# Last tail of a fused attention and FFN block: projection with centred, gamma-scaled weights and the residual summed on TensorE

## The chip, the cores and the metric

The kernel runs on one core of one Trainium2 chip. The metric is the device time of one execution in microseconds. Three runs of the kernel before gave 428.54, 428.6 and 428.6 us, median 428.6.

## The reference

The input x has 2048 rows of 128 numbers; there are 16 heads of 8 numbers each. What is computed:

```
xn  = layernorm(x)                              # no gamma, no beta
q, k, v = split(xn @ w_qkv)                     # per head
w   = relu(q k^T / sqrt(8));  w = w / (sum(w) + 1e-6)
o   = (w v) @ w_out + b_out
y   = xn + o
x1  = x + (y - mean(y)) * rsqrt(var(y) + 1e-5) * gamma + beta
z   = layernorm(x1)
out = x1 + sqrt((z @ cos(theta'))^2 + (z @ sin(phi'))^2)
```

All is fp32. theta' and phi' are the weights with their noise added.

## The kernel before

The 2048 rows are 16 tiles of 128, four tiles to a chunk (`TPC` = 4, `NC` = 4). The kernel makes four passes, one for the 512 queries of each chunk. A pass has 4 head groups of 4 heads, and a group has 16 steps, one for each tile of keys: `score_step` computes four score tiles (L961) into two of three PSUM pairs `sc0` to `sc2`, ScalarE and VectorE take their ReLU into `w_buf` (`relu_step`, L533, L536, L686, L690), and two steps later `value_step` multiplies them with the values and a column of ones into `pv0` or `pv1` (L996).

What follows the attention of a chunk (division by the sums, output projection, residual, post norm, FFN, norm of its output) is spread over the next pass as hooks: pairs `((group, step), function)` in the lists `after_pass`, on each engine its own. Every engine runs its instructions in the order in which they are written, and engines meet only at semaphores. So (2, 4) in VectorE's list of pass 1 means: behind the ReLUs of step 4 of group 2.

The last chunk has no next pass. Its end is written out as a tail in halves of two tiles each (`Part(NC - 1, 0)` and `Part(NC - 1, 1)`, 256 columns), and the engines take turns on it: ScalarE copies the sums of values to `pv_sb` (L613), TensorE transposes them (`transpose_pv`), VectorE divides (`normalise`, L699 to L701), TensorE transposes back (`transpose_o`), ScalarE copies into `oT` (L557), TensorE projects (`project_out`, L1022). From there `residual` adds `xn` (L748; `xn` holds the normalised x with b_out already added by GpSimd, L438), `post_stats` takes statistics (L756), `post_inverse` makes 1 / (var + eps) (L763 to L766), ScalarE the root (`post_root`, L562), `times_gamma` makes (y - mean) * gamma (L772), and `first_residual` x1 = that * rs + x_sb (L782; GpSimd has put x - mean + beta in `x_sb`). Then TensorE transposes x1 (L1003) and multiplies with the FFN weights (L1051), ScalarE squares (L571), VectorE adds (L836), ScalarE takes roots (L581), VectorE adds x2 (L844), and SyncE's queue stores. Meanwhile GpSimd adds the mean back (`mean_again`, L457). Between the projections and the transposes of x1 TensorE runs 20 matmuls that nobody reads (`warm_up`, L922).

An object `Own` is an engine's wait on its own last write, by a semaphore, before it reads it.

Of the kernel before, what the change touches and what calls it, by code (L numbers as in the profile page):

```python
# [44 lines left out]
STEPS = G * NT  # L45
W_STEPS = 4
WARM_UP = 12
TAIL_WARM_UP = 20
PSUM_PAIRS = 3
LAG = 2  # L50
FIRST_BOTH_LATE = ((1, 11, 13, 15), (3, 8, 10, 12, 14), (0, 3, 8, 12), (3, 8, 11, 13))
# [29 lines left out]
def block_kernel(nc, x, w_qkv, w_out, b_out, gamma, beta, theta, phi, theta_noise, phi_noise, out):  # L81
# [3 lines left out]
    with ctx:  # L85
        def sb(name, shape, dt=F32):
            return ctx.enter_context(nc.sbuf_tensor(name, shape, dt))

        def sem(name):
            return ctx.enter_context(nc.semaphore(name))  # L90
# [40 lines left out]
        angles = sb("angles", [P, 4, D])  # L131
        turns = sb("turns", [P, 2, D])
        ffn_w = sb("ffn_w", [P, 2, D])
        averager = sb("averager", [P, P])
        stats = sb("stats", [P, NT, 6])
        mv = sb("mv", [P, NT, 2])
# [93 lines left out]
        mag_ready = sem("mag_ready")  # L230
        x2_ready = sem("x2_ready")
        stored = sem("stored")

        def k_turn(c):

# [2 lines left out]
        def chunk(c):  # L238
            return bass.ds(c * TPC, TPC)
# [47 lines left out]
        def row(v, d):  # L287

            return v[:, :].unsqueeze(1).to_broadcast([P, d, D])

        with nc.Block() as block:
# [97 lines left out]
            def _(pool):  # L389
# [45 lines left out]
                pool.wait_ge(consts_loaded, 64)  # L435
                pool.wait_ge(xT_done, NC + 1)
                for c in range(NC):
                    nc.gpsimd.tensor_tensor(xn[:, chunk(c), :], xn[:, chunk(c), :], row(bout_b, TPC),  # L438
                                            ALU.add).then_inc(xb_ready, 1)
# [21 lines left out]
                def finish(part):  # L461

                    mean_again(part)
                    for n, tiles, _ in part.pieces():
                        sl = slice(tiles.start, tiles.stop)
                        pool.wait_ge(sq_ready, n + 1)
                        nc.gpsimd.tensor_tensor(mag[:, sl, :], sq[:, sl, 0, :], sq[:, sl, 1, :],  # L467
                                                ALU.add).then_inc(sum_ready, 1)
                    pool.wait_ge(mag_ready, 2 * part.n + 2)
                    pool.wait_ge(mean_back, part.n + 1)  # L470
                    nc.gpsimd.tensor_tensor(x2[:, :, :], x2[:, :, :], mag[:, :, :], ALU.add).then_inc(x2_ready, 1)  # L471


                scale_o(0, G)
                finish(Part(0))
                for c in range(1, NC - 1):
# [12 lines left out]
            def _(act):  # L489
# [134 lines left out]
            def _(dve):  # L624
# [129 lines left out]
                def post_stats(part, src):  # L754
                    for t in part.all():
                        last = nc.vector.bn_stats(stats_p[:, t, :], src[:, t, :])  # L756
                    part.chain(last)

                def post_inverse(part, norm):

                    nc.vector.memset(spare[:, :], 0.0)
                    for t in part.all():
                        last = nc.vector.bn_aggr(mv_p[:, t, :], stats_p[:, t, :])  # L763
                    part.chain(last)
                    part.chain(nc.vector.tensor_scalar_add(iv_p[:, norm, part.sl()], mv_p[:, part.sl(), 1], LN_EPS))
                    nc.vector.reciprocal(iv_p[:, norm, part.sl()],  # L766
                                         iv_p[:, norm, part.sl()]).then_inc(iv_ready[norm], 1)
# [57 lines left out]
                dve.wait_ge(xb_ready, 2 * NC)  # L825
                dve.wait_ge(consts_loaded, 64)
                for c in range(1, NC):
                    run_pass(c, after_pass(c - 1)
                             + ([((3, 7), lambda: invert_sums(NC - 1, G - 1))] if c == NC - 1 else []))

                halves = [start_chain(Part(NC - 1, 0)), start_chain(Part(NC - 1, 1))]

                def tail_sum(part, i):
                    n, (t,), _ = part.pieces()[i]
# [25 lines left out]
            def _(pe):  # L860
# [58 lines left out]
                def warm_up(n):  # L919

                    for _ in range(n):
                        nc.tensor.matmul(pv[0][:, 0:P], ident[:, :], ident[:, :], start=True, stop=True)  # L922

                pe.wait_ge(ident_ready, 1)
                warm_up(WARM_UP)
# [129 lines left out]
                def after_pass(j):  # L1055
                    part = Part(j)
                    return [((0, 12), lambda: project_out(part)),
                            ((1, 11), lambda: transpose_x1(part)), ((2, 4), lambda: ffn(part, 0)),
                            ((2, 8), lambda: ffn(part, 1))]

                def run_pass(c, hooks):

                    for s in range(STEPS):
                        score_step(c, s)
                        if s < LAG and c > 0:
                            value_step(c - 1, STEPS - LAG + s)
# [22 lines left out]
                    value_step(NC - 1, s)  # L1089

                halves = [Part(NC - 1, 0), Part(NC - 1, 1)]
                for part in halves:
                    transpose_pv(part.half, part.pv_bank, part.all())
                for stage in (transpose_o, project_out):
                    for part in halves:
                        stage(part)
                warm_up(TAIL_WARM_UP)
# [27 lines left out]
```

## Time and profile before

| | us |
|---|---|
| median of 3 runs | 428.6 |
| the profiled execution | 428.66 |
| its span (first to last instruction) | 426.8 |
| busy TensorE in a stretch of 95 us, about a pass | 95.00 |
| last matmul of the attention to the end of the span | 16.0 |
| projection of the first half ready to x1 of the second half | 5.9 |

In the rows below, times are microseconds from the span's start, and a name such as L1022 is a line of the listing. PE is TensorE, PEld its weight loads, DVE VectorE, ACT ScalarE, POOL GpSimd. A busy time that stands before x4 is that of four instructions that overlap in part, so four durations sum to more than it.

### The profile page before, as it was taken

The numbers are of one execution on the slowest core, as the hardware profiler recorded it, in microseconds if no ns is written. First come the engines' busy times: TensorE is split into PE (matmuls) and PEld (weight loads), VectorE is DVE, ScalarE is ACT, GpSimd is POOL, SyncE is SP. The second block draws the span as 40 slices with busy tenths as digits, with TensorE's granted clock in tenths as the row PEclk, the third lists the DMA queues.
The fourth block names the chain that finished last, engine by engine and source line by source line (L and its number), as shares of the span: only waits on it lengthen the run. The fifth ranks groups of instructions, "written<-read, shape, count | busy, mean of one in ns | idle before, by whom it ended". The sixth has DMA issues, their size and how long they took to land.

```text
span 426.8 us, 9025 instructions
## 1 busy us (share of the span) xinstructions
PE 415.0 (97%) x3294; PEld 122.9 (29%) x3294; DVE 332.9 (78%) x659; ACT 339.1 (79%) x595; POOL 45.9 (11%) x57
## 2 busy tenths in 40 slices
PE   7899999999999999999999999999999999999985
PEld 6333222222222322222222322222222322222244
DVE  6775778777688898777778898777778898777857
ACT  2767878788788888888888888888888888888843
POOL 4794000000000000000101000000100000000201
PEclk9999999999999999999999999999999999999999
DMA  5117841001012100101011100101012000000200
GB/s 166 25 51 148 162 111 51 2 8 43 2 51 56 26 26 13 39 2 51 26 53 54 26 27 16 35 2 51 26 51 55 2 27 2 25 2 29 66 0 26
DMA packets 11134, 17.42 MB, mean 41 GB/s; under 512 B 3092, under 2 KB 4756, under 8 KB 10708
## 3 DMA queue, kind: packets, MB, share of 16 engines
q1 hardware_dynamic: 10948, 16.70, 14.6%
q8 instruction: 29, 0.48, 0.5%
q10 hardware_dynamic: 144, 0.13, 0.2%
q14 instruction: 13, 0.11, 0.1%
HBM read 3.86 MB, written 5.10 MB: 21 GB/s over the span
## 4 chain that ended last, share of the span: by engine, by line
PE 93%; DVE 3%; ACT 2%; DMA 1%; POOL 0%; issue 0%; DVEq 0%
PE pv L996 59%; PE sc L961 27%; PE pv L1051 1%; PE pv L893 1%; PE pv L902 1%; PE pv L914 1%; DMA x_sb<-x_dram 1%; PE pv L1022 1%; ACT w_buf L536 0%; PE pv L1003 0%; DVE stats L640 0%; ACT w_buf L533 0%; DVE x L782 0%; PE sc L1051 0%; PE sc L1003 0%
## 5 line engine op out<-in xcount | busy, mean ns | idle before, releaser
L996 PE MATMUL pv<-w_buf,v_sb 128*32 128x512 f32 x2048 | 272.4, 604 | 0.0
L686 DVE TENSOR_SCALAR w_buf<-sc 128x512 f32<-128x512 f32 x256 | 176.9, 691 | 73.8 <-PE sc L961 64.9
L533 ACT ACTIVATE w_buf<-sc 128x512 f32<-128x512 f32 x256 | 153.1, 598 | 67.0 <-PE sc L961 66.5
L536 ACT ACTIVATE w_buf<-sc 128x512 f32<-128x512 f32 (+1 forms) x256 | 183.7, 718 | 0.0
L961 PE MATMUL sc<-q_rep,k_rep 32*128 32x512 f32 x1024 | 134.0, 494 | 2.3 <-ACT w_buf L533 0.9
L690 DVE TENSOR_SCALAR w_buf<-sc 128x512 f32<-128x512 f32 x182 | 123.8, 680 | 1.3 <-PE sc L961 1.3
L961 PEld LDWEIGHTS sc<-q_rep,k_rep 32*128 32x128 f32 x1024 | 52.4, 181 | 216.6 <-ACT w_buf L533 175.9
L996 PEld LDWEIGHTS pv<-w_buf,v_sb 128*32 128x32 f32 x2048 | 40.4, 108 | 66.5 <-ACT w_buf L536 34.1
L451 POOL TENSOR_TENSOR oT<-o_raw,o_scale 128x512 f32<-128x512 f32 (+1 forms) x4 | 5.1, 1282 | 164.6 <-DMA o_scale<-inverse_dram 100.7
L467 POOL TENSOR_TENSOR mag<-sq 128x256 f32<-128x256 f32 x6 | 4.4, 730 | 77.5 <-ACT sq L571 77.5
L457 POOL TENSOR_TENSOR x<-x,mv 128x512 f32<-128x512 f32 (+1 forms) x5 | 4.4, 885 | 71.2 <-DVE x L782 71.2
L922 PE MATMUL pv<-ident 128*128 128x128 f32 x64 | 9.4, 316 | 1.5 <-POOL ident L392 1.5
L922 PEld LDWEIGHTS pv<-ident 128*128 128x128 f32 x64 | 9.1, 230 | 1.5 <-POOL ident L392 1.5
L471 POOL TENSOR_TENSOR x<-x,mag 128x512 f32<-128x512 f32 x3 | 3.8, 1283 | 52.7 <-ACT mag L581 52.7
L544 ACT COPY pv_sb<-pv 128x512 f32<-128x512 f32 x15 | 8.8, 585 | 0.2
L1051 PE MATMUL pv<-ffn_w,x1T 128*128 128x256 f32 x24 | 6.8, 405 | 0.0
L659 DVE TENSOR_TENSOR q_lo<-pv,q_hi 128x512 fp32r<-128x512 f32 x4 | 2.8, 692 | 4.3 <-ACT q_hi L505 4.3
L581 ACT ACTIVATE mag<-mag,iv_p 128x128 f32<-128x128 f32 x16 | 5.4, 398 | 0.0
L397 POOL MEMSET v_sb<- 128x1472 f32 x4 | 5.3, 1334 | 0.0
L438 POOL TENSOR_TENSOR xn<-xn,bout_b 128x512 f32<-128x512 f32 x4 | 5.1, 1284 | 0.0
L441 POOL TENSOR_TENSOR x_sb<-x_sb,beta_b 128x512 f32<-128x512 f32 x4 | 5.1, 1279 | 0.0
L782 DVE SCALAR_TENSOR_TENSOR x<-y,rs_p,x_sb 128x128 f32<-128x128 f32 x16 | 5.0, 367 | 0.0
(104 smaller groups left out, 136.1 us busy)
## 6 DMA issues: line engine op xcount, KB each, us to landing
pv_dram<-pv_sb SPq DMA_DIRECT2D x15, 256.0 KB, 2.0
q_rep<-q_hi SPq DMA_DIRECT2D x30, 64.0 KB, 2.1
q_rep<-q_lo SPq DMA_DIRECT2D x30, 64.0 KB, 2.1
k_rep<-k_hi SPq DMA_DIRECT2D x6, 256.0 KB, 4.1
k_rep<-k_lo SPq DMA_DIRECT2D x6, 256.0 KB, 5.3
x_sb<-x_dram SPq DMA_DIRECT2D x3, 256.0 KB, 3.9
o_raw<-pv_dram SPq DMA_DIRECT2D x3, 256.0 KB
o_scale<-inverse_dram SPq DMA_DIRECT2D x3, 256.0 KB
```

What stands on the lines that cost most here:

```text
L397: nc.gpsimd.memset(v_sb[:, :, heads, HD + 1:VW], 0.0).then_inc(v_pad, 1)
L438: nc.gpsimd.tensor_tensor(xn[:, chunk(c), :], xn[:, chunk(c), :], row(bout_b, TPC), ALU.add).then_inc(xb_ready, 1)
L533: nc.scalar.activation(w_buf[:, s % W_STEPS, 0, :], early[:, 0, :], ACT.Relu).then_inc(relu[0], 1)
L536: nc.scalar.activation(w_buf[:, s % W_STEPS, 2:2 + n, :], late[:, 0:n, :], ACT.Relu).then_inc(relu[0], 1)
L544: nc.scalar.copy(pv_sb[:, :], bank[:, :]).then_inc(pv_out, 1)
L581: last = nc.scalar.activation(mag[:, t, :], mag[:, t, :], ACT.Sqrt, scale=iv_p[:, 1, t:t + 1])
L686: nc.vector.tensor_scalar(w_buf[:, s % W_STEPS, 1, :], early[:, 1, :], 0.0, None, ALU.max).then_inc(relu[1], 2 if both else 1)
L690: nc.vector.tensor_scalar(w_buf[:, s % W_STEPS, 3, :], late[:, 1, :], 0.0, None, ALU.max).then_inc(relu[1], 1)
L922: nc.tensor.matmul(pv[0][:, 0:P], ident[:, :], ident[:, :], start=True, stop=True)
L961: last = nc.tensor.matmul(sc[buf][:, i % 2, :], k_rep[rows, g, k * P:(k + 1) * P], q_rep[rows, g, :], start=True, stop=True)
L996: last = nc.tensor.matmul(bank[32 * i:32 * i + 32, :], v_sb[:, k, HPG * g + i, :], w_buf[:, s % W_STEPS, i, :], start=(k == 0), stop=(k == ...
L1051: last = nc.tensor.matmul(bank[:, m * 2 * D:(m + 1) * 2 * D], x1T[:, t * P:(t + 1) * P], ffn_w[:, :, :].rearrange("p c d -> p (c d)"), sta ...
```

## The change

The tail of the last chunk is computed in another way. The mean over a row of the projection is linear in its input. So TensorE gets two other right sides: `wout_tail[0]`, w_out with each row's mean taken away, and `wout_tail[1]`, the same times gamma. `x_tail[0]` and `x_tail[1]` are the last chunk's xn plus centred bias, without and with gamma. A matmul of the identity with `x_tail` opens an accumulation (`tail_x`), and the projection adds to it. One sum (in `sc2`) gives the variance, and its statistics are taken by VectorE straight from PSUM; the other (in `pv0` and `pv1`) is the centred and scaled y, from which `tail_x1` makes x1 in one instruction for each tile. ScalarE takes the root of var + eps with eps as bias, and VectorE the reciprocal. The 20 matmuls of `warm_up` in the tail are gone. The small right sides are made ahead: the means of the rows by VectorE in pass 1 (`tail_means`, a hook at (2, 4)), the rest by GpSimd behind its work on chunk 0 (`centred_tail`), and GpSimd's add of b_out to chunk 3 is left out.

```diff
+                def centred_tail():
+                    last = chunk(NC - 1)
+                    pool.wait_ge(means_ready, 1)
+                    nc.gpsimd.tensor_tensor(wout_tail[:, 0, :], wout_sb[:, :], row_means[:, 0:1].to_broadcast([P, D]),
+                                            ALU.subtract).then_inc(wout_centred, 1)
...
+                    nc.gpsimd.tensor_tensor(x_tail[:, 0, :, :], xn[:, last, :], row(bias_tail, TPC),
+                                            ALU.add).then_inc(x_tail_centred, 1)
...
-                for stage in (take_oT, post_root, take_x1T):
+                def tail_root(part):
+                    act.wait_ge(tail_var, part.half + 1)
+                    nc.scalar.activation(std_p[:, part.sl()], mv_p[:, part.sl(), 1], ACT.Sqrt,
+                                         bias=eps_col[:, :]).then_inc(tail_std, 1)
...
+                def tail_means():
+                    own = Own(dve, means_own)
+                    nc.vector.tensor_reduce(row_means[:, 0:1], wout_sb[:, :], mybir.AxisListType.X, ALU.add)
+                    own(nc.vector.tensor_reduce(row_means[:, 1:2], bout_b[:, :], mybir.AxisListType.X, ALU.add))
+                    nc.vector.tensor_scalar_mul(row_means[:, :], row_means[:, :], 1 / D).then_inc(means_ready, 1)
...
+                def tail_stats(part):
+                    dve.wait_ge(proj_done, part.n + 1)
+                    for n, t in enumerate(part.all()):
+                        last = nc.vector.bn_stats(stats_p[:, t, :], part.y_bank[:, n * P:(n + 1) * P])
+                    own[part.half](last)
...
+                def tail_x1(part):
+                    dve.wait_ge(scaled_done, part.half + 1)
+                    own[part.half].wait()
+                    for n, t in enumerate(part.all()):
+                        last = nc.vector.scalar_tensor_tensor(
+                            out=x1[:, t, :], in0=pv[part.half][:, n * P:(n + 1) * P], scalar=rs_p[:, t:t + 1],
+                            in1=x_sb[:, bass.ds(part.j * TPC + t, 1), :].rearrange("p o d -> p (o d)"),
+                            op0=ALU.mult, op1=ALU.add)
+                    last.then_inc(x1_ready, 1)
+                    dve.wait_ge(x1_ready, part.n + 1)
...
-                for stage in (residual, lambda p: post_stats(p, y), lambda p: post_inverse(p, 0), times_gamma,
-                              first_residual, lambda p: post_stats(p, x1), lambda p: post_inverse(p, 1)):
+                first, second = halves
+                tail_stats(first)
+                tail_variance(first)
+                tail_stats(second)
+                tail_inverse(first)
+                tail_variance(second)
+                tail_x1(first)
+                tail_inverse(second)
+                tail_x1(second)
+                for stage in (lambda p: post_stats(p, x1), lambda p: post_inverse(p, 1)):
...
+                def tail_x(part, which, bank):
+                    nc.tensor.matmul(bank[:, 0:part.tiles * P], ident[:, :],
+                                     x_tail[:, which, part.sl(), :].rearrange("p t d -> p (t d)"),
+                                     start=True, stop=False)
...
```

On TensorE, from the transposes of the sums of values on, the order was this (`sc` and `pv` with their buffer's number):

```order
L1003 MATMUL sc0<-ident,pv_sb 128x128 x2
L1003 MATMUL sc1<-ident,pv_sb 128x128 x2
L1003 MATMUL sc0<-ident,o_sb 128x128 x2
L1003 MATMUL sc1<-ident,o_sb 128x128 x2
L1022 MATMUL sc2<-wout_sb,oT 128x128 x4
L922 MATMUL pv0<-ident 128x128 x20
L1003 MATMUL sc0<-ident,x1 128x128 x2
```

And the same place of the changed kernel, which has one row more ahead of the transposes:

```order
L1186 MATMUL pv0<-x_tail,ident 128x256
L1093 MATMUL sc0<-ident,pv_sb 128x128 x2
L1093 MATMUL sc1<-ident,pv_sb 128x128 x2
L1186 MATMUL sc2<-x_tail,ident 128x256
L1093 MATMUL sc0<-ident,o_sb 128x128 x2
L1093 MATMUL sc1<-ident,o_sb 128x128 x2
L1196 MATMUL sc2<-wout_tail,oT 128x128 x2
L1186 MATMUL sc2<-x_tail,ident 128x256
L1196 MATMUL sc2<-wout_tail,oT 128x128 x2
L1196 MATMUL pv0<-wout_tail,oT 128x128 x2
L1186 MATMUL pv1<-x_tail,ident 128x256
L1196 MATMUL pv1<-wout_tail,oT 128x128 x2
```

The second half's projection for the statistics now stands behind a matmul of 256 columns, and four projections and one more such matmul stand where the 20 unread ones were.

On VectorE, between the division (`o_sb`) and the statistics of x1, the order was this:

```order
L748 TENSOR_TENSOR y<-sc2,xn 128x256 x2
L756 BN_STATS stats_p<-y 128x6 x4
L761 MEMSET spare 128x1
L763 BN_AGGR mv_p<-stats_p 128x2 x2
L765 TENSOR_SCALAR iv_p<-mv_p 128x2
L766 RECIPROCAL iv_p<-iv_p 128x2
...
L772 SCALAR_TENSOR_TENSOR y<-y,mv_p,gamma_b 128x128 x4
L782 SCALAR_TENSOR_TENSOR x1<-y,rs_p,x_sb 128x128 x4
```

In the changed kernel the same place holds these:

```order
L889 BN_STATS stats_p<-sc2 128x6 x2
L895 BN_AGGR mv_p<-stats_p 128x2 x2
L889 BN_STATS stats_p<-sc2 128x6 x2
L901 RECIPROCAL rs_p<-std_p 128x2
L895 BN_AGGR mv_p<-stats_p 128x2 x2
L908 SCALAR_TENSOR_TENSOR x1<-pv0,rs_p,x_sb 128x128 x2
L901 RECIPROCAL rs_p<-std_p 128x2
L908 SCALAR_TENSOR_TENSOR x1<-pv1,rs_p,x_sb 128x128 x2
```

The adds of `xn` and the multiplications by gamma are gone, and the halves are interleaved in another way.

## Rows read from the trace of the kernel before

**Rows 1.** Page, part 1: busy time and share of the span
```profile
PE 415.0 (97%) x3294; PEld 122.9 (29%) x3294; DVE 332.9 (78%) x659; ACT 339.1 (79%) x595; POOL 45.9 (11%) x57
```

**Rows 2.** Stretches: busy us of each engine, then granted clock, DMA share, GB/s
```profile
310.00:405.00 95.00, 95.00 (x784) 25.52 (x780) 76.93 (x143) 79.88 (x139) 6.34 (x6) 1.00 0.10 29
411.00:413.60 2.60, 1.51 (x9) 0.90 (x9) 1.09 (x6) 0.87 (x3) 0.00 (x0) 1.00 0.00 0
413.60:419.20 5.60, 5.60 (x49) 5.42 (x48) 4.46 (x22) 0.77 (x3) 0.00 (x0) 1.00 0.02 3
```

**Rows 3.** Timeline of the tail, TensorE and ScalarE: start, us, engine, instructions
```profile
408.01 2.78 PE L996 MATMUL pv<-w_buf,v_sb 128*32 128x512 f32 x24
411.29 0.71 PE L1003 MATMUL sc<-ident,pv_sb 128*128 128x128 f32 x4 [0.49 <-ACT pv_sb L613]
413.21 0.41 PE L1003 MATMUL sc<-ident,o_sb 128*128 128x128 f32 x2 [0.16 <-DVE o_sb L701]
413.51 1.28 PE L1022 MATMUL sc<-wout_sb,oT 128*128 128x128 f32 x8
413.66 0.36 ACT L557 COPY oT<-sc 32x256 f32<-32x256 f32 x1 [0.20 <-PE sc L1003]
414.62 4.63 PE L922 MATMUL pv<-ident 128*128 128x128 f32 x40
420.51 1.89 PE L1051 MATMUL sc<-ffn_w,x1T 128*128 128x256 f32 x8
```

**Rows 4.** Timeline of VectorE in the tail
```profile
414.26 0.42 DVE L748 TENSOR_TENSOR y<-sc,xn 128x256 f32<-128x256 f32 x1 [1.19 <-PE sc L1022]
414.89 0.42 DVE L748 TENSOR_TENSOR y<-sc,xn 128x256 f32<-128x256 f32 x1 [0.21 <-PE sc L1022]
415.35 1.01 DVE L756 BATCH_NORM_STATS2 stats_p<-y 128x6 f32<-128x128 f32 x4
416.40 0.18 DVE L763 BATCH_NORM_AGGREGATE mv_p<-stats_p 128x2 f32<-128x6 f32 x1
416.50 0.15 DVE L763 BATCH_NORM_AGGREGATE mv_p<-stats_p 128x2 f32<-128x6 f32 x1
417.45 0.17 DVE L766 RECIPROCAL iv_p<-iv_p 128x2 f32<-128x2 f32 x1
417.54 1.12 DVE L772 SCALAR_TENSOR_TENSOR y<-y,mv_p,gamma_b 128x128 f32<-128x128 f32 x4
418.58 1.61 DVE L782 SCALAR_TENSOR_TENSOR x<-y,rs_p,x_sb 128x128 f32<-128x128 f32 x4
```

**Rows 5.** Chain of waits from x1 on: start, us, what
```profile
420.24 0.44 PE sc L1003 x2
420.68 1.31 PE sc L1051 x6
```

**Rows 6.** Line L782 in the tail: shortest, median and longest in ns
```profile
L782 DVE SCALAR_TENSOR_TENSOR x<-y,rs_p,x_sb x4: 343/348/700, 418.6 to 419.5; 128x128 f32<-128x128 f32 x4
```

**Rows 7.** Timeline of GpSimd, and of VectorE beside it
```profile
419.35 0.69 POOL L457 TENSOR_TENSOR x<-x,mv 128x256 f32<-128x256 f32 x1 [15.22 <-DVE x L782]
10.39 1.04 POOL L418 TENSOR_TENSOR xn<-xn,rstd 128x512 f32<-128x512 f32 x1
10.47 0.72 DVE L671 SCALAR_TENSOR_TENSOR k_rep<-k_head,low_rows,sc 128x512 fp32r<-128x512 f32 x1
23.21 4.04 POOL L433 TENSOR_TENSOR x_sb<-x_sb,mv 128x512 f32<-128x512 f32 x4
25.43 0.69 DVE L659 TENSOR_TENSOR k_lo<-pv,k_hi 128x512 fp32r<-128x512 f32 x1 [0.39 <-ACT k_hi L501]
```

**Rows 8.** Groups of the tail: busy us, mean ns, idle before
```profile
L562 ACT ACTIVATE rs_p<-iv_p 128x2 f32<-128x2 f32 x2 | 0.4, 204 | 3.4 <-DVE iv_p L766 3.4
L581 ACT ACTIVATE mag<-mag,iv_p 128x128 f32<-128x128 f32 x4 | 1.3, 391 | 0.0
L756 DVE BATCH_NORM_STATS2 stats_p<-y 128x6 f32<-128x128 f32 x4 | 1.0, 285 | 0.1
L1022 PE MATMUL sc<-wout_sb,oT 128*128 128x128 f32 x8 | 1.3, 300 | 0.0
L1051 PE MATMUL sc<-ffn_w,x1T 128*128 128x256 f32 x8 | 1.9, 380 | 0.0
```

**Rows 9.** Timeline around step (2, 4) of pass 1, and a VectorE reduction near the start
```profile
1.50 0.22 DVE L629 TENSOR_REDUCE low_rows<-ident 128x1 f32<-128x64 f32 x1 [1.50 <-POOL ident L392]
176.61 0.69 DVE L686 TENSOR_SCALAR w_buf<-sc 128x512 f32<-128x512 f32 x1 [0.15 <-PE sc L961]
178.57 0.51 PE L961 MATMUL sc<-q_rep,k_rep 32*128 32x512 f32 x4
179.11 0.69 DVE L686 TENSOR_SCALAR w_buf<-sc 128x512 f32<-128x512 f32 x1 [1.21 <-PE sc L961]
```

**Rows 10.** Timeline of GpSimd around its new work
```profile
203.43 1.28 POOL L471 TENSOR_TENSOR x<-x,mag 128x512 f32<-128x512 f32 x1 [17.55 <-ACT mag L581]
233.59 1.28 POOL L451 TENSOR_TENSOR oT<-o_raw,o_scale 128x512 f32<-128x512 f32 x1 [28.87 <-issue]
```

More of the change, by code:

```diff
@@ L47 @@
 WARM_UP = 12
-TAIL_WARM_UP = 20
 PSUM_PAIRS = 3
@@ L133, in block_kernel @@
         ffn_w = sb("ffn_w", [P, 2, D])
+        row_means = sb("row_means", [P, 2])
+        wout_tail = sb("wout_tail", [P, 2, D])
+        bias_tail = sb("bias_tail", [P, D])
+        x_tail = sb("x_tail", [P, 2, TPC, D])
+        eps_col = sb("eps_col", [P, 1])
+        std_p = sb("std_p", [P, TPC])
         averager = sb("averager", [P, P])
@@ L232, in block_kernel @@
         stored = sem("stored")
+        means_own = sem("means_own")
+        means_ready = sem("means_ready")
+        wout_centred = sem("wout_centred")
+        bias_centred = sem("bias_centred")
+        x_tail_centred = sem("x_tail_centred")
+        tail_ready = sem("tail_ready")
+        scaled_done = sem("scaled_done")
+        eps_ready = sem("eps_ready")
+        tail_var = sem("tail_var")
+        tail_std = sem("tail_std")
+        tail_own = [sem("tail_own0"), sem("tail_own1")]
         def k_turn(c):
@@ L437, in _ @@
                 for c in range(NC):
-                    nc.gpsimd.tensor_tensor(xn[:, chunk(c), :], xn[:, chunk(c), :], row(bout_b, TPC),
-                                            ALU.add).then_inc(xb_ready, 1)
+                    if c < NC - 1:
+                        nc.gpsimd.tensor_tensor(xn[:, chunk(c), :], xn[:, chunk(c), :], row(bout_b, TPC),
+                                                ALU.add).then_inc(xb_ready, 1)
                     pool.wait_ge(x_centred, c + 1)
@@ L471, in finish @@
                     nc.gpsimd.tensor_tensor(x2[:, :, :], x2[:, :, :], mag[:, :, :], ALU.add).then_inc(x2_ready, 1)
+                def centred_tail():
[3 more added lines that the diff above has]
+                                            ALU.subtract).then_inc(wout_centred, 1)
+                    nc.gpsimd.tensor_tensor(bias_tail[:, :], bout_b[:, :], row_means[:, 1:2].to_broadcast([P, D]),
+                                            ALU.subtract).then_inc(bias_centred, 1)
+                    pool.wait_ge(wout_centred, 1)
+                    nc.gpsimd.tensor_tensor(wout_tail[:, 1, :], wout_tail[:, 0, :], gamma_b[:, :],
+                                            ALU.mult).then_inc(tail_ready, 1)
+                    pool.wait_ge(bias_centred, 1)
+                    nc.gpsimd.tensor_tensor(x_tail[:, 0, :, :], xn[:, last, :], row(bias_tail, TPC),
+                                            ALU.add).then_inc(x_tail_centred, 1)
+                    pool.wait_ge(x_tail_centred, 1)
+                    nc.gpsimd.tensor_tensor(x_tail[:, 1, :, :], x_tail[:, 0, :, :], row(gamma_b, TPC),
+                                            ALU.mult).then_inc(tail_ready, 1)
+                nc.gpsimd.memset(eps_col[:, :], LN_EPS).then_inc(eps_ready, 1)
                 scale_o(0, G)
                 finish(Part(0))
+                centred_tail()
                 for c in range(1, NC - 1):
@@ L613, in _ @@
                     nc.scalar.copy(pv_sb[:, part.cols()], pv[1][:, part.cols()]).then_inc(pv_out, 1)
-                for stage in (take_oT, post_root, take_x1T):
+                def tail_root(part):
+                    act.wait_ge(tail_var, part.half + 1)
+                    nc.scalar.activation(std_p[:, part.sl()], mv_p[:, part.sl(), 1], ACT.Sqrt,
+                                         bias=eps_col[:, :]).then_inc(tail_std, 1)
+                act.wait_ge(eps_ready, 1)
+                for stage in (take_oT, tail_root, take_x1T):
                     for part in halves:
@@ L827, in _ @@
                 for c in range(1, NC):
-                    run_pass(c, after_pass(c - 1)
+                    run_pass(c, after_pass(c - 1) + ([((2, 4), tail_means)] if c == 1 else [])
                              + ([((3, 7), lambda: invert_sums(NC - 1, G - 1))] if c == NC - 1 else []))
                 halves = [start_chain(Part(NC - 1, 0)), start_chain(Part(NC - 1, 1))]
+                own = [Own(dve, tail_own[0]), Own(dve, tail_own[1])]
+                def tail_stats(part):
[3 more added lines that the diff above has]
+                    own[part.half](last)
@@ new lines, in tail_variance, with tail_inverse @@
+                def tail_variance(part):
+                    for t in part.all():
+                        last = nc.vector.bn_aggr(mv_p[:, t, :], stats_p[:, t, :])
+                    last.then_inc(tail_var, 1)
+                def tail_inverse(part):
+                    dve.wait_ge(tail_std, part.half + 1)
+                    own[part.half].later(nc.vector.reciprocal(rs_p[:, part.sl()], std_p[:, part.sl()]))
+                def tail_x1(part):
[8 more added lines that the diff above has]
+                    dve.wait_ge(x1_ready, part.n + 1)
@@ L917, in project_v, with warm_up @@
                     last.then_inc(v_done, 1)
-                def warm_up(n):
+                def warm_up(n, bank):
                     for _ in range(n):
-                        nc.tensor.matmul(pv[0][:, 0:P], ident[:, :], ident[:, :], start=True, stop=True)
+                        nc.tensor.matmul(bank[:, 0:P], ident[:, :], ident[:, :], start=True, stop=True)
                 pe.wait_ge(ident_ready, 1)
-                warm_up(WARM_UP)
+                warm_up(WARM_UP, pv[0])
                 transpose_first()
@@ L1091, in _, with project_tail @@
                 halves = [Part(NC - 1, 0), Part(NC - 1, 1)]
+                first, second = halves
+                def tail_x(part, which, bank):
+                    nc.tensor.matmul(bank[:, 0:part.tiles * P], ident[:, :],
+                                     x_tail[:, which, part.sl(), :].rearrange("p t d -> p (t d)"),
+                                     start=True, stop=False)
+                def project_tail(part, which, bank, done):
+                    if which == 0:
+                        pe.wait_ge(oT_ready, part.n + 1)
+                        pe.wait_ge(oT_three, 1)
+                    for n, t in enumerate(part.all()):
+                        last = nc.tensor.matmul(bank[:, n * P:(n + 1) * P], oT[:, t * P:(t + 1) * P],
+                                                wout_tail[:, which, :], start=False, stop=n == part.tiles - 1)
+                    last.then_inc(done, 1)
+                pe.wait_ge(tail_ready, 2)
+                tail_x(first, 1, pv[0])
                 for part in halves:
                     transpose_pv(part.half, part.pv_bank, part.all())
[L1094 to L1097, printed above, removed]
+                tail_x(first, 0, first.y_bank)
+                transpose_o(first)
+                transpose_o(second)
+                project_tail(first, 0, first.y_bank, proj_done)
+                tail_x(second, 0, second.y_bank)
+                project_tail(second, 0, second.y_bank, proj_done)
+                project_tail(first, 1, pv[0], scaled_done)
+                tail_x(second, 1, pv[1])
+                project_tail(second, 1, pv[1], scaled_done)
                 for part in halves:
```

2 lines of the change are left out of this document (1 added, 1 removed).

## The prediction

> **What bounds the kernel now.** I read the page's busy times first. TensorE is busy for 97% of the span, VectorE for 78%, GpSimd for 11% [rows 1]. Then the stretches: a whole pass shows 95.00 us of busy TensorE in 95 us at a granted clock of 1.00, so the passes are bound by TensorE, and work on other engines is free there as long as TensorE doesn't wait for it. The stretch 411.0 to 413.6 shows 1.51 us of 2.6 [rows 2]: from the last attention matmul on (408.01 + 2.78 = 410.79) the engines take turns. Third, the timeline of that tail. The projection of the first half is ready when VectorE's first add starts, at 414.26; VectorE then works, but for a wait of 0.21, to the end of L782 at 418.58 + 1.61 = 420.19 [rows 4]. TensorE shows as busy in that time, but 414.62 to 419.25 is the unread warm-up [rows 3]. So there VectorE alone sets the end. Behind it stands the chain of x1: transposes at 420.24, FFN matmuls at 420.68 [rows 5], the rest to the span's end at 426.8. That chain starts at the second half of x1, and the change doesn't touch it. What the change is worth is how much sooner than 420.19 that x1 is there.
>
> **The part that is replaced.** Before: 420.19 - 414.26 = 5.93 us. It holds two adds (414.26 to 415.31, with a wait for the second half's projection), four statistics (415.35 to 416.36), two variances with reciprocals (to 417.62), four multiplications by gamma and four L782 [rows 4].
>
> After, on VectorE, by the same rows. The start stays 414.26: the first projection needs the same `oT`, and what stands new ahead of it on TensorE is covered (below).
> - First statistics: four took 1.01 [rows 4] at 285 ns each [rows 8], a distance of (1.01 - 0.285) / 3 = 0.24, so 0.53 for two: to 414.79. Own wait 0.04 (416.36 to 416.40). Two aggregations 0.25 (416.40 to 416.65): 414.83 to 415.08.
> - Second statistics: they need the second projection. TensorE: L1022's last instruction of the first half starts about 413.90, for it lasts 275 ns and the add started at 414.26 some 0.09 behind its end. Instructions follow each other at 0.11 us for 128 columns (4.63 us less one duration, over 39) and at 0.216 for 256 columns (1.89 - 0.38 = 1.51 over 7) [rows 3, 8]; a matmul in fp32 is two instructions. So the identity matmul starts at 414.01, and the four instructions of the second projection at 414.44 to 414.76, ending at 415.04, seen by VectorE at 415.13. Before it was 414.89; now it is 0.24 later, yet VectorE is free only at 415.10. Statistics 415.13 to 415.66.
> - Reciprocal of the first half: 0.04 + 0.17, to 415.87. ScalarE's root has had since 415.08; it is not late.
> - Aggregation of the second half 415.80 to 416.05, laid over the reciprocal as L763 is laid over L766.
> - x1 of the first half: two instructions at a distance of 0.28 with 0.35 for the last (1.12 for four L772; 343 ns for L782 alone [rows 4, 6]), 0.63: 416.07 to 416.70.
> - Reciprocal of the second half 416.74 to 416.91, own wait, x1 of the second half 416.94 to 417.57.
>
> After: 417.57 - 414.26 = 3.31. The gain is 5.93 - 3.31 = 2.62 us.
>
> **Does TensorE keep up?** Behind the second projection come two scaled projections (4 instructions each) with an identity matmul between: first scaled one 414.87 to 415.47, needed at 416.07; the second starts at 415.73 and ends at 416.33, needed at 416.94. It has 0.5 us of room. The 20 warm-up matmuls are no loss of work, and the transposes of x1 no longer queue behind them. The identity matmul ahead of `transpose_pv` falls into the idle 0.49 us before 411.29 [rows 3], of which it needs 0.43; the one ahead of `transpose_o` into the time in which VectorE divides.
>
> **The price of what no row shows.** Statistics with a PSUM source: the nearest rows are adds and multiply-adds with one PSUM operand. L671 took 0.72 for 512 columns with one, 0.18 more than its columns at 1.05 ns each (L659's 0.69 less L748's 0.42, over 256 columns); L782 from SBUF is 0.343, 0.21 more than its 128 columns [rows 4, 6, 7]. So at one end 0.03 less for each of the six new PSUM readers that follow one another on the path, 0.2 us gained. At the other end such readers don't overlap: 0.07 more for each pair of x1 and 0.04 for each pair of statistics, 0.2 us lost. I take 0, in the middle, since a difference of 0.03 between two unlike lines carries little. The root with a bias column: no row has one; between L562 (204 ns) and L581 with its scale column (391) [rows 8]. At 0.39 the first root ends at 415.50, needed at 415.70; the second at 416.47, needed at 416.74. Zero either way.
>
> **A stall that goes, or not.** Three of the tail's L782 took about 345 ns and one 700, while GpSimd's `mean_again` ran from 419.35 to 420.04 [rows 6, 7]. Now that GpSimd work starts about 0.13 behind the first half's x1, at 416.83, and would lie over both instructions of the second half. But the new instruction reads PSUM and one SBUF tile, and L671 with such operands took 0.72 with L418 beside it on GpSimd, L659 0.69 within L433's 4.04 us [rows 7]: no such stall. I count none; if it comes it is 0.35 us, once. The Trainium skill (SBUF — State Buffer, section "SBUF: two separate sides") says that VectorE and GpSimd share a pair of ports as an exclusive lock, against VectorE instructions with two SBUF inputs. By that rule the stall goes too, and the trace agrees with its 700 against 345 ns.
>
> **What is put into the passes.** `tail_means`: two reductions and a small multiply. L629 took 0.22 for 64 columns, so some 0.28 for 128 [rows 9]; with the own wait about 0.75 us on VectorE, ahead of the L686 at 176.61. That L686 then ends at 177.9, its partner at 178.5. TensorE reads neither before 178.57, where it issues the next scores, and VectorE was idle for 1.21 us before 179.11 [rows 9], since TensorE's own FFN matmuls give it that time. Cost 0; without this cover up to 0.6. GpSimd's five instructions: two of 1.28 (like L471) and three under 0.4 are 3.7 us from 204.7 on; its next work is at 233.59 [rows 10]. It loses one of 1.28 in pass 0. While it runs VectorE has only ReLUs, which read PSUM as L671 does. Cost 0.
>
> **The sum.** 428.66 of the profiled execution - 2.62 = 426.04. That execution lies 0.06 above the median, so 426.0 as a median.
>
> **The rivals.**
> 1. VectorE doesn't get all of it: the stall of 0.35 comes back, over x1 of the second half: 426.0 + 0.35 = 426.4 (with the 0.2 of readers that don't overlap 426.6). For it: L782's 700 ns [rows 6]. Against: the two rows with a PSUM operand [rows 7].
> 2. TensorE becomes the bound: instructions that add to one bank don't overlap, as if each took its whole 275 or 379 ns. Then 16 x 0.275 + 4 x 0.379 = 5.9 us from 413.51 put the last scaled projection at 419.4 and x1 at 420.1, no gain: 428.6. Against: L996 accumulates too, and its 24 took 2.78 us with 600 ns each.
> 3. The clock, late: without the warm-up the granted clock falls to 1.2 GHz around the transposes of x1. Then 0.44 + 1.31 [rows 5] double: 426.0 + 1.75 = 427.8.
> 4. The clock, early; the slower case. If it falls from 411 on, where TensorE is the least busy, the six groups behind 413.57 take 5.2 instead of 2.6 us, the eight transposes ahead some 0.8 more, so the last scaled projection is there at about 419.9 and x1 at 420.5; with the chain's 1.75 the time is 428.7 + 0.3 + 1.75 = 430.7. It decides from the point where the clock is at half before 413.6. Against: the row of 411.0 to 413.6 has the clock at 1.00 with 1.51 us of 2.6 busy [rows 2], and that stretch gets busier now, not less. New idle time is only 416.4 to 416.7 and some 0.6 us between the transposes of x1.
>
> The Trainium skill (TensorE: Matmul & The Clock Gate, section "Why this matters for your kernels") warns that an array left idle between bursts falls back to half clock, which speaks against taking the warm-up away. What it would do here is rivals 3 and 4; no stretch of this trace with matmuls in the tail shows a fall.
>
> **Chances.** Forecast 0.68; rival 1 0.14; better than forecast by up to 0.5, if waits close more tightly, 0.04; rival 2 0.05; rival 3 0.05; rival 4 0.04. A change under 0.2% (0.86 us) can't be told from none with this kernel. The forecast, its better variant and rival 1 are faster (0.86), of rival 3 (0.8 to 0.9 us) a part, so 0.87; same 0.08; slower 0.05. The range holds forecast and rival 1 with the bounds of the unknown costs, 425.4 to 426.9.
>
> **What would show it.** In the changed profile the first statistics start at about 3.5 us behind the last attention matmul; x1 of the second half ends some 3.3 us after that; both x1 pairs show durations near 350 ns; TensorE's last scaled projection ends before the second pair; the clock stands at 1.00 to the last matmul; no idle time of TensorE around the new hook in pass 1; and from x1 to the end it is 6.6 us as before. I am wrong if TensorE, not VectorE, is what the x1 pairs wait for, or if TensorE waits within the passes (95 us no longer hold 95.00 busy).

## The result and the profile after

The changed kernel takes 425.92 us (median of 4, 425.84 to 426.02), the kernel before 428.6 us beside it: ratio 0.9938, 95% interval [0.9924, 0.9952], 2.68 us less. The forecast was 426.0 us. The profiled execution took 425.92 us with a span of 424.1.

VectorE in the tail of the changed kernel (timeline: start, us, engine, line, operation); these rows answer to [rows 4]:

```profile
414.27 0.49 DVE L889 BATCH_NORM_STATS2 stats_p<-sc 128x6 f32<-128x128 f32 x2 [1.25 <-PE sc L1196]
414.80 0.25 DVE L895 BATCH_NORM_AGGREGATE mv_p<-stats_p 128x2 f32<-128x6 f32 x2
415.15 0.49 DVE L889 BATCH_NORM_STATS2 stats_p<-sc 128x6 f32<-128x128 f32 x2
415.68 0.17 DVE L901 RECIPROCAL rs_p<-std_p 128x2 f32<-128x2 f32 x1
415.76 0.23 DVE L895 BATCH_NORM_AGGREGATE mv_p<-stats_p 128x2 f32<-128x6 f32 x2
415.95 0.61 DVE L908 SCALAR_TENSOR_TENSOR x<-pv,rs_p,x_sb 128x128 f32<-128x128 f32 x2
416.59 0.17 DVE L901 RECIPROCAL rs_p<-std_p 128x2 f32<-128x2 f32 x1
416.86 0.61 DVE L908 SCALAR_TENSOR_TENSOR x<-pv,rs_p,x_sb 128x128 f32<-128x128 f32 x2
```

The start is the old one (414.27, before 414.26). The last row ends at 416.86 + 0.61 = 417.47, where L782 had ended at 420.19. So the part that took 5.93 us takes 3.20, 2.73 us less, and the spans differ by 2.7. Everything behind x1 kept its length: 424.1 - 417.5 = 6.6 us, as before.

VectorE isn't quite without a gap: its first aggregations end at 414.80 + 0.25 = 415.05, and the second statistics start at 415.15. The chain that ended last (start, us, what) comes to VectorE from TensorE at that point and stays on VectorE to the end of x1, but for its issue times:

```profile
414.67 0.46 PE sc L1196 x4
415.15 0.51 DVE stats_p L889 x2
```

TensorE in the same tail, for [rows 3]:

```profile
410.69 0.70 PE L1186 MATMUL pv<-x_tail,ident 128*128 128x256 f32 x2
411.25 0.71 PE L1093 MATMUL sc<-ident,pv_sb 128*128 128x128 f32 x4
414.51 0.61 PE L1196 MATMUL sc<-wout_tail,oT 128*128 128x128 f32 x4
414.95 0.61 PE L1196 MATMUL pv<-wout_tail,oT 128*128 128x128 f32 x4
415.40 0.60 PE L1186 MATMUL pv<-x_tail,ident 128*128 128x256 f32 x2
415.83 0.61 PE L1196 MATMUL pv<-wout_tail,oT 128*128 128x128 f32 x4
416.62 0.44 PE L1093 MATMUL sc<-ident,x 128*128 128x128 f32 x2 [0.18 <-DVE x L908]
417.53 0.44 PE L1093 MATMUL sc<-ident,x 128*128 128x128 f32 x2 [0.47 <-DVE x L908]
```

The identity matmul ahead of the transposes delayed nothing (411.25, before 411.29). The last scaled projection ends at 416.44, 0.42 us ahead of the L908 that reads it. The matmuls of one accumulation follow each other like any others: four instructions take 0.61 us, as at the 0.11 us step of the unread ones in [rows 3]. TensorE idles for 0.18 and 0.47 us around the transposes of x1. The clock (stretches: busy time of PE, PEld, DVE, ACT and POOL, then granted clock, DMA share, GB/s) stayed at 1.00 to the last matmul, and the first stretch is busier than its counterpart in [rows 2] (2.23 of 2.6 us, before 1.51):

```profile
411.00:413.60 2.60, 2.23 (x13) 1.15 (x11) 1.10 (x6) 0.83 (x3) 0.00 (x0) 1.00 0.00 0
413.60:417.00 3.40, 3.22 (x22) 2.75 (x22) 2.42 (x13) 0.95 (x3) 0.27 (x1) 1.00 0.00 0
417.00:420.00 3.00, 2.22 (x11) 1.61 (x10) 2.75 (x18) 2.16 (x6) 0.95 (x2) 1.00 0.00 0
```

### The profile page after: what moved, and what is told of

Read it like the earlier page. It is cut to its first block, busy times and chain, and to the rows that moved or that the text cites. A ratio compares the mean times of both kernels' runs of the same rounds, so it can differ in the third digit from the quotient of the medians.

```text
span 424.1 us, 8977 instructions
## 1 busy us (share of the span) xinstructions
PE 413.5 (97%) x3270; PEld 120.9 (29%) x3270; DVE 330.9 (78%) x652; ACT 339.3 (80%) x595; POOL 48.3 (11%) x62
## 4 chain that ended last, share of the span: by engine, by line
PE 93%; DVE 2%; ACT 2%; DMA 1%; POOL 0%; issue 0%; DVEq 0%
PE pv L1086 60%; PE sc L1051 27%; PE pv L1141 2%; PE pv L983 1%; PE pv L992 1%; PE pv L1004 1%; PE pv L1112 1%; DMA x_sb<-x_dram 1%; ACT w_buf L573 0%; PE pv L1093 0%; DVE stats L683 0%; ACT w_buf L570 0%; PE sc L1141 0%; PE pv L972 0%; ACT L585 0%
## 5 line engine op out<-in xcount | busy, mean ns | idle before, releaser
L1012 PE MATMUL pv<-ident 128*128 128x128 f32 x24 | 5.1, 408 | 1.5 <-POOL ident L408 1.5
L1012 PEld LDWEIGHTS pv<-ident 128*128 128x128 f32 x24 | 5.0, 318 | 1.5 <-POOL ident L408 1.5
L983 PE MATMUL pv<-xT,w 128*128 128x512 f32 x8 | 4.5, 641 | 0.3 <-ACT xT L534 0.2
```

What stands on the lines that cost most here:

```text
L983: nc.tensor.matmul(k_bank[c], w3[:, 1, :], xT[:, c * CW:(c + 1) * CW], start=True, stop=True).then_inc(k_done, 1)
L1012: nc.tensor.matmul(bank[:, 0:P], ident[:, :], ident[:, :], start=True, stop=True)
```

## The experiments

Each median is compared with the kernel before, run beside it on the same chip: 428.64 us (29 runs) for b_nowarm, b_pool_late, a_warm and a_gamma_dve, 428.78 us (9 runs) for a_gamma_warm, a_again, a_pe4 and a_sq, 428.61 us (7 runs) for a_hook. Times of profiled executions are compared from the start of the tail on, since the executions enter the passes up to 0.6 us apart (a group of transposes of xn near the start begins on TensorE at 11.31 to 11.94 us).

### The kernel before without its warm-up (b_nowarm)

```diff
-                warm_up(TAIL_WARM_UP)
```

> The kernel before without the 20 unread matmuls in its tail. Theory A (they hold the clock over the 4.4 us in which TensorE would else be idle, 414.8 to 419.24): the granted clock falls before the transposes of x1, and transposes and FFN, 1.75 us at full clock, take up to twice that: up to 430.3 us. Theory B (they do nothing here): 428.6 us, clock 1.00 to the last matmul. Either way the 2.7 us gained by the change don't come from taking them out, which would need 425.9 here.

Measured: 430.29 us (6 runs, 429.58 to 430.53), ratio 1.0033 [1.0022, 1.0044]. TensorE's timeline and some of the stretches:

```profile
419.29 0.69 PE L1003 MATMUL sc<-ident,x 128*128 128x128 f32 x2 [4.45 <-DVE x L782]
420.30 0.69 PE L1003 MATMUL sc<-ident,x 128*128 128x128 f32 x2 [0.32 <-DVE x L782]
420.78 3.23 PE L1051 MATMUL sc<-ffn_w,x1T 128*128 128x256 f32 x8
```

```profile
414.00:416.00 2.00, 0.84 (x7) 0.60 (x5) 1.41 (x5) 0.07 (x1) 0.00 (x0) 1.00 0.00 0
416.00:418.00 2.00, 0.00 (x0) 0.00 (x0) 1.82 (x14) 0.41 (x2) 0.00 (x0) 0.66 0.00 0
418.00:420.00 2.00, 0.69 (x2) 0.29 (x2) 1.96 (x7) 0.00 (x0) 0.59 (x1) 0.50 0.00 0
```

TensorE has no work for 4.45 us from 413.56 + 1.28 = 414.84 on. The clock falls to 0.50, which is 1.2 GHz, within that gap: the mean of 0.66 over 416 to 418 puts the fall at about 416.6, an estimate from the two levels 1.00 and 0.50. The FFN matmuls (eight instructions) take 3.23 us instead of 1.89. Theory A holds: the matmuls that nobody reads were worth 430.29 - 428.64 = 1.65 us by the medians, and about 1 us in the two shortest of the six runs (429.58 and 429.70). Their removal by itself is no part of the gain. The Trainium skill (TensorE: Matmul & The Clock Gate, section "Why this matters for your kernels") warns of idle gaps between bursts of matmuls. This trace agrees: the clock fell within the gap of 4.45 us.

### The kernel before with GpSimd's work later (b_pool_late)

```diff
+                pool.wait_ge(x1_ready, NC + 1)
                 for half in range(2):
                     mean_again(Part(NC - 1, half))
```

> The kernel before, with GpSimd adding the mean back for both halves only when x1 of both is done. Theory (GpSimd's work stalled one L782 for 0.35 us, as both operands of it come from SBUF): all four L782 of the tail take about 345 ns, time 428.25 us. Rival (the 700 ns have another cause): one L782 still takes 700 ns, 428.6 us.

Measured: 428.19 us median (12 runs), 0.45 less, ratio 0.9994 [0.9985, 1.0003]. The interval alone doesn't tell it from no change, since two of the runs lie near 429.7. The other ten lie between 428.01 and 428.44, and the 26 of the kernel before that are not near 429.6 between 428.38 and 428.83. The rows decide (L783 is L782 moved by a line):

```profile
419.14 1.26 DVE L783 SCALAR_TENSOR_TENSOR x<-y,rs_p,x_sb 128x128 f32<-128x128 f32 x4
```

Four in 1.26 us, where [rows 4] have 1.61: the 0.35 us of stall are gone when GpSimd works later. In the changed kernel they are gone although GpSimd still works beside (line L908 in the tail: shortest, median and longest in ns; and GpSimd's row):

```profile
L908 DVE SCALAR_TENSOR_TENSOR x<-pv,rs_p,x_sb x4: 341/346/350, 416.0 to 417.1; 128x128 f32<-128x128 f32 x4
```

```profile
416.73 0.61 POOL L474 TENSOR_TENSOR x<-x,mv 128x256 f32<-128x256 f32 x1 [12.36 <-DVE x L908]
```

The profiled execution of this variant is one of its two long ones (429.75 us), and shows why. TensorE's projections (L1023, 1.28 us in the kernel before) and its warm-up (L923, there 4.63 us), with four stretches:

```profile
413.56 1.79 PE L1023 MATMUL sc<-wout_sb,oT 128*128 128x128 f32 x8
415.14 5.78 PE L923 MATMUL pv<-ident 128*128 128x128 f32 x40
```

```profile
411.00:413.00 2.00, 1.02 (x6) 0.60 (x6) 0.97 (x6) 0.56 (x2) 0.00 (x0) 1.00 0.00 0
413.00:415.00 2.00, 1.84 (x11) 1.60 (x11) 0.54 (x2) 0.73 (x2) 0.00 (x0) 0.78 0.00 0
415.00:417.00 2.00, 2.00 (x11) 2.00 (x11) 1.43 (x7) 0.00 (x0) 0.00 (x0) 0.50 0.00 0
417.00:419.00 2.00, 2.00 (x18) 2.00 (x17) 1.86 (x14) 0.41 (x2) 0.00 (x0) 0.86 0.03 8
```

The clock falls between 413 and 415, behind a stretch in which TensorE has 1.02 us of work in 2, and is back before 419. The kernel before has such executions too: of the 29 beside these variants three took 429.6 us, at a mean granted clock of 0.996 where the others have 0.997 to 1.000. Its profiled execution has the same sparse stretch without a fall, so what decides between executions stays open.

### The changed kernel with the warm-up put back (a_warm)

```diff
                 project_tail(second, 1, pv[1], scaled_done)
+                for _ in range(20):
+                    nc.tensor.matmul(sc[1][:, 1, 0:P], ident[:, :], ident[:, :], start=True, stop=True)
```

> The changed kernel with 20 unread matmuls put back, behind the last scaled projection. Theory (TensorE ends its projections at 416.44, only 0.2 us before the first transposes of x1, so there is no room for warm-up): the 20 take 4.4 us, to 420.6, transposes and FFN come 3.0 to 3.6 us later, 428.9 to 429.5 us. Rival (the warm-up was hidden and is neutral): 425.9 us.

Measured: 429.71 us (8 runs, 429.51 to 430.11), ratio 1.0023 [1.0013, 1.0034]. TensorE ends the 40 instructions at 416.06 + 4.63 = 420.69, and the transposes, due at 416.4, start at 420.53. The warm-up is in the way now: the gap that it filled is gone. It costs 3.7 us against the changed kernel, a little more than the 3.0 to 3.6 expected.

### Gamma and centring left to VectorE (a_gamma_dve, a_gamma_warm)

The first variant undoes the half of the change that makes the second set of sums: `x_tail` holds xn plus b_out, x1 is made from y as before, and the second set of projections goes with both of its identity matmuls, also the one ahead of the transposes. The other is the same plus the nine unread matmuls of the last two lines.

```diff
...
-                    dve.wait_ge(scaled_done, part.half + 1)
-                    own[part.half].wait()
+                    for n, t in enumerate(part.all()):
+                        last = nc.vector.scalar_tensor_tensor(out=y[:, t, :], in0=part.y_bank[:, n * P:(n + 1) * P],
+                                                              scalar=mv_p[:, t, 0:1], in1=gamma_b[:, :],
+                                                              op0=ALU.subtract, op1=ALU.mult)
+                    own[part.half](last)
...
-                                                wout_tail[:, which, :], start=False, stop=n == part.tiles - 1)
+                                                wout_sb[:, :], start=False, stop=n == part.tiles - 1)
...
-                project_tail(first, 1, pv[0], scaled_done)
-                tail_x(second, 1, pv[1])
-                project_tail(second, 1, pv[1], scaled_done)
+                for _ in range(9):
+                    nc.tensor.matmul(pv[0][:, 0:P], ident[:, :], ident[:, :], start=True, stop=True)
```

> The changed kernel with half of its idea: the residual still comes by an identity matmul and the statistics from PSUM, but w_out is neither centred nor scaled, the second set of projections is left out, and VectorE makes (y - mean) * gamma with four instructions. Theory (VectorE alone sets the end): two pairs of 0.61 us and two own waits of 0.04 come back, x1 of the second half at 418.76 instead of 417.47, 427.2 us; so of the 2.7 us gained 1.3 come from the scaled sums and 1.4 from residual, statistics, root and order. Rival (TensorE is what x1 waits for, so leaving out its second projections pays for the VectorE work): 426.0 to 426.4 us.

Measured: 428.29 us (11 runs, 427.09 to 428.92), ratio 0.9992 [0.9983, 1.0]. Both theories miss. VectorE did as the first says in kind: L911, the second half's x1, ends at 418.38, and the part started at 414.15, so 4.23 us against 3.20. That is 1.03 us more, where 1.3 was expected. But the FFN matmuls behind it are slow, after a gap in front of the transposes:

```profile
417.07 0.44 PE L1096 MATMUL sc<-ident,x 128*128 128x128 f32 x2 [2.08 <-DVE x L911]
418.43 0.44 PE L1096 MATMUL sc<-ident,x 128*128 128x128 f32 x2 [0.92 <-DVE x L911]
418.71 3.20 PE L1144 MATMUL sc<-ffn_w,x1T 128*128 128x256 f32 x8
```

```profile
417.00:419.00 2.00, 1.01 (x6) 0.75 (x7) 1.86 (x9) 0.47 (x2) 1.16 (x2) 1.00 0.00 0
419.00:421.00 2.00, 2.00 (x7) 1.59 (x6) 1.82 (x14) 1.05 (x3) 0.07 (x1) 0.53 0.00 0
```

The clock fell behind idle times of 2.08 and 0.92 us, in the middle of busy work. One run of the eleven, 427.09 us, has about the time that the theory gave (427.2), and a mean granted clock of 0.998 where the other ten have 0.989 to 0.996. The second variant tests this reading.

> The variant with gamma and centring on VectorE, with 9 unread matmuls put into the 2.1 us in which TensorE was idle ahead of the first transposes of x1. Theory (its 428.3 us were 1.0 us of VectorE work and 1.3 us of half clock under the FFN): clock 1.00 there, L-rows of the FFN matmuls near 1.9 us for eight instead of 3.2, 427.0 us. Rival (the time is lost elsewhere): stays at 428.3 us.

Measured: 427.06 us (5 runs, 426.99 to 427.12), ratio 0.996 [0.9947, 0.9972]; the FFN matmuls are back at full speed:

```profile
415.06 2.17 PE L1213 MATMUL pv<-ident 128*128 128x128 f32 x18
418.93 1.89 PE L1144 MATMUL sc<-ffn_w,x1T 128*128 128x256 f32 x8
```

So 1.2 of the 428.29 were the clock, and the gap of 2.08 us is what mattered: the one of 0.92 between the transposes is still there. With the clock held, gamma and centring on TensorE are worth 427.06 - 426.03 = 1.03 us, and the rest of the change 428.78 - 427.06 = 1.72. Part of that rest is the stall of 0.35 us, for no L911 takes more than 352 ns; residual, statistics, root and order were not told apart.

The first variant also has an instruction with a PSUM operand beside GpSimd's work, the second of these two pairs:

```profile
415.79 0.58 DVE L906 SCALAR_TENSOR_TENSOR y<-sc,mv_p,gamma_b 128x128 f32<-128x128 f32 x2
417.13 0.59 DVE L906 SCALAR_TENSOR_TENSOR y<-sc,mv_p,gamma_b 128x128 f32<-128x128 f32 x2
417.19 0.61 POOL L474 TENSOR_TENSOR x<-x,mv 128x256 f32<-128x256 f32 x1 [13.03 <-DVE x L911]
```

It takes no longer than the pair that GpSimd leaves alone (0.59 against 0.58).

### The changed kernel again (a_again)

> The changed kernel itself, many executions beside those of before. Theory (in its tail TensorE is never idle for more than about half a microsecond behind 413.6, so the clock stays up in every execution): all within 0.2 us of 425.9, without the executions about 1 us longer that the kernel before shows (3 of 29 near 429.6). Rival (its tail is as exposed to the clock as others): some executions at 427 to 428 us.

Measured: 426.03 us (5 runs, 425.85 to 426.17), ratio 0.9936 [0.9924, 0.9949]. The highest lies 0.27 above 425.9, a little more than expected. With the four runs of the result none of nine is about 1 us longer, and none of the 14 runs of a_pe4, a_hook and a_sq has a mean granted clock below 0.998. Of the kernel before it was three of the 45 beside all variants, so these are too few to call the changed kernel safe from it; the busier stretch ahead of 413.6 speaks for it, and that is an argument only.

### TensorE's room (a_pe4)

```diff
+                for _ in range(4):
+                    nc.tensor.matmul(sc[1][:, 1, 0:P], ident[:, :], ident[:, :], start=True, stop=True)
                 tail_x(second, 1, pv[1])
```

> The changed kernel with 4 unread matmuls (0.87 us) ahead of the second half's identity matmul and scaled projection. Theory (TensorE has 0.3 to 0.4 us of room: the last scaled projection ends at 416.44 and VectorE takes it at 416.86): it ends at 417.3, x1 of the second half waits and comes 0.45 to 0.55 later, 426.4 us. Rival A (VectorE alone binds, more room): 425.9 us. Rival B (TensorE binds already, no room): 426.8 us.

Measured: 426.49 us (5 runs, 426.34 to 426.94), 0.46 above the changed kernel beside it. The profiled execution is the one of 426.94 us; it entered the passes 0.5 us later than that of the changed kernel (that group begins at 11.94, there at 11.43), which is no part of the tail. VectorE now waits for TensorE:

```profile
415.92 1.06 PE L1212 MATMUL sc<-ident 128*128 128x128 f32 x8
416.81 0.60 PE L1186 MATMUL pv<-x_tail,ident 128*128 128x256 f32 x2
417.11 0.17 DVE L901 RECIPROCAL rs_p<-std_p 128x2 f32<-128x2 f32 x1
417.89 0.61 DVE L908 SCALAR_TENSOR_TENSOR x<-pv,rs_p,x_sb 128x128 f32<-128x128 f32 x2 [0.61 <-PE pv L1196]
```

The four matmuls hold the identity matmul back by 416.81 - 415.92 = 0.89 us. The distance from L901 to L908 is 0.78 us instead of 0.27, so 0.51 of the 0.89 came out: 0.38 was room.

### The means without cover (a_hook)

```diff
-                    run_pass(c, after_pass(c - 1) + ([((2, 4), tail_means)] if c == 1 else [])
+                    run_pass(c, after_pass(c - 1) + ([((3, 9), tail_means)] if c == 1 else [])
```

> The changed kernel with the means of the rows taken at step (3, 9) of pass 1, where no FFN matmuls of TensorE stand beside them, instead of (2, 4). Theory (a delay of 0.6 us of one ReLU meets about 0.45 us of slack, since TensorE needs the early ReLU of a step only with the late scores of the next): TensorE waits 0.1 to 0.2 us once, 426.1 us, and the idle time of VectorE a few steps on makes up for the rest. Rival A (no slack): TensorE loses 0.6 us, 426.5 us. Rival B (all hidden there too): 425.9 to 426.0 us and no wait of TensorE.

Measured: 426.23 us (4 runs, 426.13 to 426.27), 0.2 to 0.3 above the two medians of the changed kernel. The runs overlap with those of a_again (up to 426.17), so the times alone don't show it, but the rows do. TensorE's four score matmuls ahead of the late ReLU, and the next four:

```profile
209.69 0.79 PE L1051 MATMUL sc<-q_rep,k_rep 32*128 32x512 f32 x4
211.40 0.51 PE L1051 MATMUL sc<-q_rep,k_rep 32*128 32x512 f32 x4
```

They took 0.79 instead of 0.51: TensorE stood for 0.28 us inside the group. It was not made up at the next group (211.40, in the changed kernel 211.12, both with the earlier ones at 208.25). At (2, 4) the same work cost nothing (the changed kernel's rows, answering to [rows 9]; TensorE's next scores 0.07 us sooner than before):

```profile
176.32 0.28 DVE L874 TENSOR_REDUCE row_means<-wout_sb 128x1 f32<-128x128 f32 x1
176.90 0.68 DVE L729 TENSOR_SCALAR w_buf<-sc 128x512 f32<-128x512 f32 x1
178.50 0.50 PE L1051 MATMUL sc<-q_rep,k_rep 32*128 32x512 f32 x4
```

### A version that beats both (a_sq)

ScalarE does what is shown below in place of VectorE's `tail_stats` and `tail_variance`, and the second half's two identity matmuls stand ahead of the `transpose_o` of the first and of the second half.

```diff
+                    for n, t in enumerate(part.all()):
+                        last = nc.scalar.activation(sq[:, t, 0, :], part.y_bank[:, n * P:(n + 1) * P], ACT.Square,
+                                                    accum_out=ssq[:, t:t + 1])
...
+                    nc.scalar.activation(std_p[:, part.sl()], ssq[:, part.sl()], ACT.Sqrt,
+                                         bias=eps_col[:, :], scale=1 / D).then_inc(tail_std, 1)
```

> A version meant to be faster: since the projection is centred, its variance is the mean of squares, which ScalarE takes with Square and a sum per row, then the root, for both halves; VectorE loses four statistics and four aggregations. TensorE does the second half's two identity matmuls earlier, between the transposes. Theory (VectorE's work sets the end, and ScalarE is idle there): squares of the first half 414.35 to 414.95, root to 415.3, second half to 416.2, x1 of the second half at 417.05 instead of 417.47, 425.5 us, now bound by ScalarE. Rival (each square with a sum costs 0.4 us or more, ScalarE is slower than what it replaces): 426.0 to 426.4 us.

Measured: 425.62 us (5 runs, 425.46 to 425.71), ratio to before 0.9926 [0.9913, 0.9938]. Its runs don't overlap with those of the changed kernel beside it (425.85 to 426.17), though the two ratios' intervals do. ScalarE's rows, and the two x1 pairs:

```profile
414.45 0.28 ACT L656 ACTIVATE sq<-sc 128x128 f32<-128x128 f32 x1 [0.20 <-PE sc L1199]
414.62 0.19 ACT L656 ACTIVATION_READ_ACCUMULATOR sq<-sc 128x1 f32 x1
415.94 0.29 ACT L660 ACTIVATE std_p<-ssq,eps_col 128x2 f32<-128x2 f32 x1
415.70 0.61 DVE L915 SCALAR_TENSOR_TENSOR x<-pv,rs_p,x_sb 128x128 f32<-128x128 f32 x2
416.62 0.61 DVE L915 SCALAR_TENSOR_TENSOR x<-pv,rs_p,x_sb 128x128 f32<-128x128 f32 x2
```

The second root ends at 416.23 and the first half's x1 at 416.31, so ScalarE and VectorE now end together. From the first square to the end of x1 it is 417.23 - 414.45 = 2.78 us, 0.42 less than 3.20, and the time is 0.4 us less. What the new place of the identity matmuls adds to that was not tried by itself.

## Why the prediction was right

**What bounds.** The part on VectorE between the first projection and x1 was the whole of it: it is 2.73 us shorter, its start moved by 0.01, and what follows kept its length. The one place where TensorE sets the time, the second projection, was forecast too: VectorE free at 415.10 and served at 415.13, in the trace 415.05 and 415.15.

**The replaced part.** Forecast 3.31 us, measured 3.20. The terms: second statistics at 415.13 (415.15), reciprocal 415.70 (415.68), first x1 416.07 (415.95), second x1 416.94 (416.86). Two errors partly cancel, and that is luck. The first x1 came 0.12 sooner than forecast. About half of this is that I let it wait for the second half's aggregation to end, but it doesn't read it, and L908 starts while L895 still runs (415.95, against 415.76 + 0.23 = 415.99); the rest is a few hundredths in reciprocal and aggregation. Against it, the step from the end of the second reciprocal to the second x1 was put at 0.03 and took 0.10 (416.76 to 416.86).

**TensorE's room.** Forecast 0.5, seen 0.42 in the profile and 0.38 in a_pe4. The scaled sums end at 416.44, forecast 416.33.

**Unknown prices.** Statistics from PSUM took 290 ns (285 from SBUF) and L908 346 (L782 without the stall 343 to 348), so the zero that I took stands; the bound of 0.2 either way was wide. The root with a bias column took 295 ns, inside its bounds, and was hidden as said.

**The stall.** It went, and b_pool_late shows that GpSimd had made it. That it is the PSUM operand which frees the new instruction was argued from two rows; that L908 takes 346 ns while GpSimd runs agrees with it, and so does L906 in a_gamma_dve. No variant changed the operand alone.

**In the passes.** The hook cost nothing at (2, 4), as said; the first ReLU behind it ended at 177.58, forecast 177.9. GpSimd's five instructions took 3.8 us (forecast 3.7). The price without cover was bounded at 0.6 and measured 0.28. One sign that I named was a bad one: "95 us hold 95.00 busy" can't show such a stall, for a_hook's stretches read 25.00 of 25.00 over it. It shows in the duration of the group, which is the sign to look at; in the changed kernel it is 0.50.

**The rivals.** Rival 2 is out: 0.61 us for four instructions of one sum. Rivals 3 and 4 didn't come in this kernel. But I weighed them too lightly as mechanisms. The weak step is "no stretch of this trace with matmuls in the tail shows a fall": true of the one trace, while three other executions of the same kernel show one by their times and clocks. Rival 3's 1.75 was an upper end (1.65 in b_nowarm, 1.2 in a_gamma_dve). Rival 4's size, 4.7 us, has nothing to bear it out: in b_pool_late the clock fell early, was back before 419, and the time was about 1.5 us longer than that of the ten shorter runs. What kept rival 3 off is that the second set of projections fills the place of the warm-up until 416.4: without it the clock fell (a_gamma_dve), and with unread matmuls in its place it didn't (a_gamma_warm). That x1 comes 2.7 us sooner should help too, and is an argument only. "The 20 warm-up matmuls are no loss of work" holds only together with that.

## What to carry to other kernels

In a tail where engines take turns, cost the change on the engine that has no gaps, row by row with the waits on its own writes, and then ask of each other engine how much room it has; that sum came to 3.31 us where 3.20 were measured. Matmuls that do work can take the place of ones that only hold the clock, but a cut that opens a gap of two microseconds on TensorE can give its gain back behind it (a_gamma_dve gave back 1.2). Put a small job beside a neighbour's extra work, as the hook at (2, 4) is: the same job cost 0.28 us where no such work stood.

## What was not expected of the hardware

The clock needs no gap of 4.45 us to fall. In b_nowarm it was down about 1.8 us into that gap, by the estimate above. In a_gamma_dve it fell behind 2.08 and 0.92 us of idle time, and then while TensorE was fully busy (0.53 over 419 to 421), in ten of eleven executions as their times and mean clocks read. In b_pool_late it fell with no idle time above 0.65 us, behind a stretch with 1.02 us of work in 2, in two of twelve executions. And a square with a sum per row on ScalarE brings a second instruction of 0.19 us, ACTIVATION_READ_ACCUMULATOR; at 128 columns the two stand for 0.28 + 0.19 us, overlapping in part.
